# Expert layers of a six-layer network: tokens sorted by expert into 7 blocks of 128, results stored in two transfers

## The reference

```
x = x + 0.5 * ffn(ln(x));  x = x + linear(ln(x));  x = x + 0.5 * ffn(ln(x))
x = x + 0.5 * experts(ln(x));  x = x + attn(ln(x));  x = x + 0.5 * experts(ln(x))
```

```
probs = softmax(q k^T * 8**-0.5)                  # 16 heads, 256 x 256 per sequence
x = layer_norm(src + (probs v) @ Wo + bo)
expert_idx = floor(x @ router_w + router_b) mod 4
for e in range(4):
    y = relu(x @ W1[e] + b1[e]) @ W2[e] + b2[e]
    ff_out += where(expert_idx == e, y, 0)
return layer_norm(x + ff_out)
```

## Time and profile before

| | |
|---|---|
| runs | 1931.28, 1931.81, 1939.92 us |
| profiled execution, its time | 1933.48 us |
| its span | 1931.3 us |
| TensorE matmul busy | 1437.2 us (74%), 10336 matmuls |
| TensorE weight load busy | 860.4 us (45%), beside the matmuls |
| VectorE busy | 1356.9 us (70%) |
| ScalarE busy | 724.2 us (37%) |
| GpSimd busy | 615.0 us (32%) |
| mean granted clock of TensorE | 0.864 |
| DMA | 62.16 MB |

### The profile page before, as it was taken

One profiled execution on the slowest core, in us unless ns is written; L12 is line 12 of the kernel. 1 busy time (PEld: TensorE's weight loads), 2 busy tenths in 40 slices (PEclk: granted clock), 3 DMA queues, 4 the chain that ended last, 5 costly groups with the idle time before them and its releaser, 6 DMA issues.

```text
span 1931.3 us, 30180 instructions
## 1 busy us (share of the span) xinstructions
PE 1437.2 (74%) x10336; PEld 860.4 (45%) x10336; DVE 1356.9 (70%) x3522; ACT 724.2 (37%) x1329; POOL 615.0 (32%) x464
## 2 busy tenths in 40 slices
PE   3667667656643557988899996665467889989997
PEld 3334334333431223555555664444123455555665
DVE  6699999999873646766776456884665567767554
ACT  1233323333110234555555531222043455555642
POOL 3245445545552201222121123664121122321211
PEclk9887888788755578999999997787576999999999
DMA  4000000000002212211120000001221102210000
GB/s 143 0 1 1 1 0 0 1 0 1 1 2 66 74 61 68 68 51 51 35 68 3 1 1 1 1 0 39 85 75 51 58 28 68 67 52 18 24 12 11
DMA packets 73541, 62.16 MB, mean 32 GB/s; under 512 B 4920, under 2 KB 66488, under 8 KB 73272
## 3 DMA queue, kind: packets, MB, share of 16 engines
q1 hardware_dynamic: 73408, 60.48, 10.0%
HBM read 32.61 MB, written 27.79 MB: 31 GB/s over the span
## 4 chain that ended last, share of the span: by engine, by line
PE 51%; DVE 27%; issue 12%; POOL 4%; DMA 2%; SPq 2%; ACT 1%; DVEq 1%; POOLq 0%; ACTq 0%
PE bank L1073 12%; PE bank L1065 11%; PE bank L1087 7%; DVE DD L1349 6%; PE bank L1103 4%; DVE NM L1578 4%; PE bank L1116 3%; PE bank L955 2%; PE bank L1125 2%; DVE A L1360 2%; PE bank L1136 1%; DVE YB L1491 1%; PE bank L1131 1%; PE bank L1199 1%; POOL rs L582 1%
## 5 line engine op out<-in xcount | busy, mean ns | idle before, releaser
L1578 DVE TENSOR_REDUCE NM<-bank 128x2 f32<-128x512 f32 x512 | 342.5, 685 | 270.2 <-PE bank L1116 269.3
L836 ACT ACTIVATE PBS<-bank 128x512 f32<-128x512 f32 x512 | 289.4, 597 | 393.1 <-PE bank L1103 392.9
L1073 PEld LDWEIGHTS bank<-W,HB 128*128 128x128 f32 x2048 | 264.1, 191 | 157.2 <-issue 135.6
L582 POOL TENSOR_TENSOR rs<-ve,half 128x4 f32<-128x4 f32 x88 | 90.2, 1025 | 707.4 <-DVE ve L1518 587.8
L1073 PE MATMUL bank<-W,HB 128*128 128x128 f32 x2048 | 272.4, 276 | 24.6 <-DVE YB L1491 24.6
L1065 PE MATMUL bank<-XT,W 128*128 128x512 f32 x512 | 284.8, 638 | 1.1 <-ACT HB L808 1.1
L1349 DVE TENSOR_TENSOR_SCAN DD<-bank,I 128x512 f32<-128x512 f32 x192 | 227.1, 1209 | 11.6 <-PE bank L943 9.2
L808 ACT ACTIVATE HB<-bank,W 128x512 f32<-128x512 f32 x256 | 176.5, 690 | 129.3 <-PE bank L1065 128.3
L943 PE MATMUL bank<-STK,SEL 128*128 128x256 bf16 (+1 forms) x512 | 87.5, 281 | 132.3 <-DVE DD L1349 130.7
L1116 PE MATMUL bank<-KS,QS 48*128 48x256 bf16 x1024 | 113.0, 303 | 79.9 <-DVE NM L1578 51.9
L616 POOL TENSOR_TENSOR A<-DD,SS 128x512 f32<-128x512 f32 x64 | 98.6, 1541 | 171.3 <-DVE DD L1349 171.2
(11 more groups left out here) (211 smaller groups left out, 2321.0 us busy)
## 6 DMA issues: line engine op xcount, KB each, us to landing
QS<-scr_q SPq DMA_DIRECT2D x64, 192.0 KB
KS<-scr_k SPq DMA_DIRECT2D x64, 192.0 KB
scr_q<-PQ SPq DMA_DIRECT2D x32, 192.0 KB, 2.2
scr_k<-PQ SPq DMA_DIRECT2D x32, 192.0 KB, 2.2
scr_q<-PQ SPq DMA_DIRECT2D x32, 128.0 KB, 2.1
scr_k<-PQ SPq DMA_DIRECT2D x32, 128.0 KB, 2.1
X<-in_x SPq DMA_DIRECT2D x8, 256.0 KB, 6.6
W<-in_w SPq DMA_DIRECT2D x8, 256.0 KB, 8.3
```

The costliest lines, as they stand in the source:

```text
L582: pool.tensor_tensor(rs_[:, :], ve_[:, :], half[:, 0:ve_.shape[1]], ALU.pow).then_inc(rstd_sem, 1)
L836: act.activation(PB[i % PB_SLOTS][:, :, :], bank[1 + i % 2][:, :].rearrange("p (k t) -> p k t", k=2), ACT.Exp).then_inc(A.e, 1)
L1073: last = pe.matmul(bank[7][:, k * P:(k + 1) * P], HB[e % 2][:, q, k * P:(k + 1) * P], W2[:, e, q, :], start=(q == 0), stop=(q == CH - 1))
L1578: dve.tensor_reduce(NM[:, 2 * b + qt, h:h + 3:2], bank[3 + i % 2][:, :].rearrange("p (u t) -> p u t", u=2), AX_X, ALU.max, negate=True).th ...
```

## The change

The experts no longer work on all 512 tokens with each expert. The tokens of a group are sorted by expert into 7 blocks of 128 tokens. Blocks 0 to 3 belong to the four experts and use the weights that stand in SBUF (resident blocks). An expert with more than 128 tokens fills further blocks, of which there are three (overflow blocks); (512 - 4) // 128 = 3 is the largest number that can be needed. What weights an overflow block needs is known only at run time, so they are fetched.

- At the start SyncE packs the weights and biases of each expert into a table in HBM, `scr_w`: for each expert 128 rows of 1156 numbers.
- VectorE's `choose` takes the place of `masks`, in slot 26 and not 27, behind the new `take(., 0)`. It ends with one comparison that gives `hot`, one column for each expert. TensorE's `count_ranks` in slot 29 (five small products with a triangle and with ones) counts the rank of each token in its expert and the tokens of each expert. VectorE's `positions` in slot 31 (14 small operations) works out the row of each token (POS) and the rows of the three overflow blocks' weights (WIX).
- In the next step Pool scatters the four tiles of XS into `scr_x` by POS (four indirect transfers), SyncE loads it back sorted as XD, TensorE transposes its seven blocks in slot 15, and ScalarE copies them to XT. Pool also gathers the overflow blocks' weights from `scr_w` into WK (three indirect transfers).
- In the odd slots from 17 on TensorE makes `up` of a block (four products of 128 columns) and `down` of the block before (four accumulating ones); ScalarE makes the Relu of a block in four operations. `take(., 0)` in slot 26 adds the biases of the resident blocks, `take(., 1)` in slot 1 of the following step those of the overflow blocks. SyncE stores the results of the two parts to `scr_y` by separate transfers: the one of the resident blocks behind slot 26's take, that of the overflow blocks behind slot 1's.
- Pool gathers the results back in token order into YG (four indirect transfers), and VectorE adds them to XS in slot 10 of the step with `fin`.
- The loop over the full steps is written out. Twenty-two constants and a running sum of the identity are set by VectorE when the engines' program comes to the first expert layer's setup, which stands between the linear-attention layer and the second feed-forward layer. The buffers KQV of the attention lie over WK, some semaphores of the feed-forward layer and the attention are shared, and one lead of the attention moves from slot 26 to 28.

The diff, cut to its core:

```diff
-UNITS = [None] * SLOTS_H
-for _e in range(EXPERTS):
-    for _k in range(CH):
-        for _kind, _slot in (("W1", 8 * _e + 2 * _k - 2), ("W2", 8 * _e + 2 * _k + 7)):
-            UNITS[_slot % SLOTS_H] = (3 + _slot // SLOTS_H, _kind, _e, _k)
...
+OVER = (N - EXPERTS) // P
+BLOCKS = EXPERTS + OVER
...
+def first_slot(b):
+    return 17 + 2 * b
...
+            for e in range(EXPERTS):
...
+                sp.dma_start(scr_w[r, 0:W2_AT], W1[:, e, :]).then_inc(E.packed, 16)
+                sp.dma_start(scr_w[r, W2_AT:B1_AT],
+                             W2[:, e, :, :].rearrange("p k c -> p (k c)")).then_inc(E.packed, 16)
...
+                    if fin:
+                        sp.wait_ge(E.yused, 2 * (c - 3))
+                        sp.dma_start(scr_y[EXPERTS * P:, :].rearrange("(b p) c -> p b c", p=P),
+                                     YB[:, EXPERTS:, :]).then_inc(E.ystored, 16)
...
+                    if exp:
+                        sp.wait_ge(E.scattered, 64 * (c - 2))
...
+                        sp.dma_start(XD[:, :, :], scr_x.rearrange("(b p) c -> p b c", p=P)).then_inc(E.sorted, 16)
...
+                    if exp:
+                        sp.wait_ge(E.yused, 2 * (c - 2) - 1)
...
+                        sp.dma_start(scr_y[0:EXPERTS * P, :].rearrange("(b p) c -> p b c", p=P),
+                                     YB[:, 0:EXPERTS, :]).then_inc(E.ystored, 16)
...
+                    if exp:
+                        pool.wait_ge(E.pos, c - 2)
...
+                        for t in range(TP):
+                            pool.indirect_dma_start(
+                                out=scr_x, out_offset=bass.IndirectOffsetOnAxis(ap=POS[other][:, t:t + 1], axis=0),
+                                in_=XS[other][:, t, :], in_offset=None).then_inc(E.scattered, 16)
+                    if fin:
...
+                        for t in range(TP):
+                            pool.indirect_dma_start(
+                                out=YG[:, t, :], out_offset=None, in_=scr_y,
+                                in_offset=bass.IndirectOffsetOnAxis(ap=POS[par][:, t:t + 1], axis=0)
...
+                    if exp:
...
+                        for k in range(OVER):
+                            pool.indirect_dma_start(
+                                out=WD[:, k, :], out_offset=None, in_=scr_w,
+                                in_offset=bass.IndirectOffsetOnAxis(ap=WIX[other][:, k:k + 1], axis=0)
+                                ).then_inc(E.weights, 16)
...
+                        if exp and i in (15, 16):
...
+                            act.activation(XT[:, at:to], bank[6 + u][:, 0:to - at], ACT.Copy).then_inc(E.xt, 1)
+                        if exp and i in range(first_slot(0), first_slot(BLOCKS), 2):
+                            relu(n - 3, (i - first_slot(0)) // 2)
...
-                def unit(p, kind, e, k):
...
-                    if kind == "W1":
...
-                        pe.matmul(bank[6][:, :], W1[:, e, k * P:(k + 1) * P], XT[:, :], start=True,
-                                  stop=True).then_inc(E.h, 1)
-                        return
...
+                def up(p, b):
...
+                    if b == EXPERTS:
+                        pe.wait_ge(E.weights, 16 * OVER * (c + 1))
+                    for k in range(CH):
+                        w = W1[:, b, k * P:(k + 1) * P] if b < EXPERTS else WD[:, b - EXPERTS, k * P:(k + 1) * P]
+                        last = pe.matmul(bank[6][:, k * P:(k + 1) * P], w, XT[:, b * P:(b + 1) * P], start=True, stop=True)
...
+                def down(p, b):
...
+                    pe.wait_ge(E.relu, c * BLOCKS + b + 1)
+                    if b == 0:
+                        pe.wait_ge(E.xt, 2 * c + 2)
+                    if b == EXPERTS:
+                        pe.wait_ge(E.yused, 2 * c + 1)
+                    for k in range(CH):
+                        at = W2_AT + k * P
+                        w = W2[:, b, k, :] if b < EXPERTS else WD[:, b - EXPERTS, at:at + P]
+                        last = pe.matmul(bank[7][:, (b % EXPERTS) * P:(b % EXPERTS + 1) * P], HB[b % 2][:, k, :], w,
+                                         start=(k == 0), stop=(k == CH - 1))
+                    last.then_inc(E.y, 1)
...
+                def count_ranks():
...
+                    pe.matmul(bank[0][:, 0:n], below[:, :], h, start=True, stop=False)
+                    for t in range(1, TP + 1):
+                        last = pe.matmul(bank[0][:, t * EXPERTS:n], allone[:, :], h[:, 0:n - t * EXPERTS],
+                                         start=False, stop=(t == TP))
...
+                            b2 = (i - first_slot(0)) // 2
+                            if exp and 0 <= b2 < BLOCKS:
+                                up(n - 3, b2)
+                            if exp and 0 < b2 <= BLOCKS:
+                                down(n - 3, b2 - 1)
+                            if exp and i == 15:
...
+                                        last = pe.transpose(bank[6 + u][:, k * P:(k + 1) * P], XD[:, at + k, :], ident)
+                                    last.then_inc(E.turned, 1)
...
+                        if post and i == 29:
...
-                            pe.wait_ge(A.x1, c - 1)
-                            turn(XS[par], E.turned)
+                            pe.wait_ge(E.hot, c - 1)
...
+                            count_ranks()
...
+                def take(p, u):
...
+                        dve.tensor_tensor(YB[:, 0:EXPERTS, :], tiles(7), R[:, k:k + EXPERTS, :],
...
+                        dve.wait_ge(E.y, c * BLOCKS + BLOCKS)
+                        dve.wait_ge(E.weights, 16 * OVER * (c + 1))
+                        dve.tensor_tensor(YB[:, EXPERTS:BLOCKS, :], tiles(7)[:, 0:OVER, :], WD[:, :, B2_AT:WROW],
+                                          ALU.add).then_inc(E.yused, 1)
...
+                def choose(p, par):
...
-                    for e in range(EXPERTS):
-                        last = dve.tensor_scalar(MK[par][:, e, :], key[2][:, :], float(e), None, ALU.is_equal)
-                    last.then_inc(E.mask, 1)
+                    dve.tensor_tensor(hot[:, 0:TP, :], over(key[2][:, :].unsqueeze(2), [P, TP, EXPERTS]),
+                                      expert_no[:, :, :], ALU.is_equal).then_inc(E.hot, 1)
+                    link.close()
...
+                def positions(p, par):
...
+                    dve.wait_ge(E.rank, c + 1)
+                    ranks = bank[0][:, 0:TP * EXPERTS].rearrange("p (t e) -> p t e", e=EXPERTS)
+                    counts = bank[0][:, TP * EXPERTS:(TP + 1) * EXPERTS]
+                    link(dve.tensor_tensor(full[:, :, :], over(counts.unsqueeze(2), [P, EXPERTS, OVER]),
+                                           filled[:, :, :], ALU.is_gt))
+                    link(dve.tensor_reduce(extra[:, :], full[:, :, :], AX_X, ALU.add))
...
+                    dve.tensor_scalar(WIX[par][:, :], owner[:, :], part_no[:, 0:1], None, ALU.add)
...
+                    dve.tensor_copy(POS[par][:, :], spot[:, :]).then_inc(E.pos, 1)
...
-                        if fin and i == 6:
-                            take(n - 4, 3)
-                        if fin and i == 7:
-                            gather(n - 4, par, 3)
+                        if fin and i == 1:
+                            take(n - 4, 1)
+                        if fin and i == 10:
+                            dve.wait_ge(E.back, 64 * (c - 3))
+                            if later(c - 4):
+                                dve.wait_ge(E.norm, c - 4)
+                            dve.tensor_tensor(AC[:, :, :], XS[par][:, :, :], YG[:, :, :], ALU.add).then_inc(E.acc, 1)
...
-                        if exp and i == 14:
-                            take(n - 3, 0)
...
-                        if exp and i == 17:
-                            gather(n - 3, other, 0)
-                        if exp and i == 22:
-                            take(n - 3, 1)
-                        if exp and i == 23:
-                            gather(n - 3, other, 1)
...
-                        if post and i == 27:
-                            masks(n - 2, par, (c - 2) * 4 - 2)
-                        if exp and i == 30:
-                            take(n - 3, 2)
-                        if exp and i == 31:
-                            gather(n - 3, other, 2)
+                        if exp and i == 26:
+                            take(n - 3, 0)
+                        if post and i == 26:
+                            choose(n - 2, par)
+                        if post and i == 31:
+                            positions(n - 2, par)
```

279 lines of the change are left out of this document (176 added, 103 removed).

## The result

The changed kernel takes 2003.97 us, the median of four runs (2003.24 to 2005.84). Its time over that of the kernel before is 1.0362, with a 95% interval of 1.0335 to 1.0389: slower by 71 us, in the direction forecast, at nearly twice the size (+37). It lies inside the range given (1885 to 2040) and outside the narrower one that the forecast gave for itself (1945 to 1995). The profiled execution has a span of 2001.5 us against 1931.3, and a mean clock of 0.768 against 0.864. TensorE's matmuls are busy for 1323.9 us, 113 less than before.

What follows compares the result with a forecast made beforehand. TensorE bounds full steps now; without expert work, a chain through one PSUM bank would pace the first half. First layer +14.9, second +19.9, constants +2.5 made +37: 1969 us, range 1885 to 2040 (forecast's own 1945 to 1995).

Steps and rivals of the forecast that it cites:

- What bounds, first half: Slots 0 to 15 of a full step: without expert work, a chain through one PSUM bank paces it; 37.2 us.
- less 1.3: First half of a full step: 1.3 us taken off because the step is entered at the full clock.
- Second half: Slots 16 to 31 of a full step: 27.8 us with VectorE's stalls, plus 2.4 for lost clock, giving 30.2.
- the stall in slot 28: Maxima of slot 28 wait for both reduces, take and choose: 3.3 us exposed on TensorE.
- Full steps together: Each full step goes from 61.5 to 67.4 us, +5.9, four times in each layer: +23.6 per layer.
- Tails: Ends of layers: -4.7 us for the sorted-load step; then 0 in the first layer, +5 in the second.
- The step behind the last maxima: First step after the last maxima, paced by exponentials and one block per pair: 39.3 us, -7.
- The constants: 22 memsets and a few small VectorE operations between the linear layer and second ffn: +2.5 us.
- The steps that only choose: Steps that only choose: +2 us, from positions and choose ahead of the reduce, less one W1 unit.
- Pool late: Rival, chance 0.14: at 2.3 us per transfer, qkr and all behind it come 6 us late; 2035 us.
- TensorE's bound: Rival, chance 0.03: TensorE stays the bound, so 16.7 us go from each of 16 passes; 1665 us.
- The clock holds: Rival, chance 0.22: halves at their floors, 29.8 and 27.8, make a full step 57.6 us; total 1883 us.

Runs made afterwards that it cites:

- the first experiment: Changed kernel plus one unread 512-column TensorE product in each odd slot 1 to 13 of steps 2 to 7: 1892.37 us, ratio 0.9789 to the kernel before.

## Why the prediction was right, and where it was too low

**What bounds, first half.** Right, and its cause is shown: the half went to 39.2 us at a clock of 0.61 where 37.2 at 0.6 to 0.75 was forecast, and giving TensorE work took it to 30.0 with all waits in place. What was mis-sized is the base. Of the two measured stretches without expert work I took the shorter, 37.7 at 0.68; with the other, 39.5 at 0.59, the same sum gives 39.0. That they differ at all is the clock, as the 32.0 at 0.93 shows, and the changed kernel's clock of 0.61 is that of the longer one. The step was entered at the full clock, as the term "less 1.3" has it; whether that gave anything no run separates. Neither of the forecast waits ahead of it is by itself what lowered the clock: without the wait for POS in slot 1 the half had 0.58, and without the dip of slot 28 it had 0.61.

**Second half.** 30.2 forecast, 29.4 measured (30.8 in step 6). Its sum of 27.8 at the full clock is what the first experiment shows (27.9). Of the stall in slot 28, put at 3.3, the later `choose` gave 2.1 back at the full clock and 1.6 more in clock; of the 2.7 for `positions`, its removal gave 2.0 there. The 2.4 that I had added for lost clock came as 1.5. The reason that I gave for them, that a stall costs clock, holds only in part: the same wait in slot 28 cost none in the first experiment.

**Full steps together.** +5.9 was forecast eight times, +7.1 to +9.3 came: 16 us of the 33 that were missing. The steps with `exp` but no `fin` (+8.3 and +9.3) have a first half of 40.3 and 41.2 us, and I had given them the value of the others; they are the ones entered at the lower level (0.59 us for the transposes of slot 1, 0.38 in the others). Step 6 (+8.4 twice) has a second half of 30.8, with a longer dip behind slot 28.

**Tails.** Here the step of the sum that failed is the last group. For the second layer behind 1909.6, -4.7 and +5 were put and -2.6 and +11.6 came: 36.2 to 33.6 us (31.5 forecast, whose terms as given add up to 31.2), then 46.7 to 58.3. After, in time order, TensorE and then Pool and VectorE:

```profile
1942.06 1.16 PE L1172 MATMUL bank<-WK,HB 128*128 128x128 f32 x8 [0.23 <-ACT HB L898]
1954.80 1.76 PE L1278 MATMUL bank<-W,XD 128*128 128x128 f32 x7 [11.59 <-DMA XD<-scr_x]
1956.61 2.07 PE L1158 MATMUL bank<-XT,W 128*128 128x128 f32 x8
1960.00 2.05 PE L1158 MATMUL bank<-XT,W 128*128 128x128 f32 x8 [1.32 <-ACT HB L898]
...
1976.10 1.16 PE L1172 MATMUL bank<-WK,HB 128*128 128x128 f32 x8 [0.34 <-ACT HB L898]
```

```profile
1980.62 1.04 POOL L714 DMA_INDIRECT YG<-scr_y,POS  x1 [17.23 <-DMA scr_y<-YB]
```

```profile
1988.27 0.69 DVE L1781 TENSOR_TENSOR AC<-XS,YG 128x512 f32<-128x512 f32 x1 [10.42 <-DMA YG<-scr_y,POS]
```

The way from POS to the sorted load is paid for each group, the last one too; I had counted it once, in the step ahead, and for the last group only store and gathers. From POS (1944.3) to the transposes it is 10.5 us, close to the 4.6 + 2.2 + 3 of the forecast. The seven blocks take from 1956.6 to 1977.3, which is 20.6 and not 16.1: the first three start 3.4, 3.5 and 2.9 us apart, since behind 11.6 idle us the clock is at its lower level, the later ones 2.45. Store and gathers take 11 us from 1977.3 to 1988.3, against 9.3. In the first layer the lead steps of the attention filled part of this, but not all: -7.6 came where -11.7 was put.

**The step behind the last maxima.** -7 forecast, -4.9 measured (46.3 to 41.4).

**Small terms.** The constants, +2.5, cost nothing: all up to the first expert layer took 0.6 us less. The steps that only choose, +2, took +3.7 and +1.1. The second layer's lead steps gave +3.5 that no step of the sum had, and whose cause is not shown.

**Rivals.** Pool late: out, with 7.09 us to spare and six more transfers free. TensorE's bound: out. The clock holds: it did not, but it gives the right price of a full step: with the clock held by hand that is 57.9, and the rival had 57.6. That its total of 1883 stands beside 1892 is luck in part: the products also took 16 us off the two steps that only choose, for which the rival had +4, and the tails came about as much worse than it had them.

**The skill's rules.** The Trainium skill (TensorE: Matmul & The Clock Gate, "Part 1: The HAM clock gate") calls the half rate the default that activity releases; by that rule the half from which TensorE's work was taken could lose the full clock, and the traces agree: 0.61 without, 1.00 with the products that nobody reads. Pool's transfers took 0.93 to 1.09 us each with VectorE busy beside them, and not near the 2.3 us at which I had put them under the shared port. The Trainium skill (SBUF — State Buffer, "Who interferes with whom") says of `tensor_reduce` that on this chip it never contends for that port. I had left that out: beside the eleven transfers of the step shown, reduces are 4.8 of VectorE's 8.4 busy us, so that this case hardly tests the lock.

## What to carry to other kernels

Work that fills an engine's gaps on a chain of hand-overs may be holding its clock up; before it is taken out or pushed together, look for a stretch of the same kernel that lacks it and read its time and its clock there. Then price what is left at both levels: here the sum of 29.8 was the answer with the clock (30.0), and the two stretches of 37.7 and 39.5 held the one without it (39.2) between them. An idle stretch of the other engine is not room for new work if what ends it is a link of the chain, and a transfer that is hidden in the steady state is paid in full for the last group.

## What the runs showed of the hardware

- One unread product of 1.02 to 1.13 us in each of seven gaps took the clock of the half from 0.61 to 1.00 and a step from 68.6 to 57.9 us. With 8 columns in place of 512 it left the clock of step 2 at 0.59, against 0.94 and 0.95.
- A W2 unit of 8 columns took 1.04 us at the full clock, one of 128 columns 1.05, eight matmuls each: fewer columns made it no shorter.
- In a full step an indirect transfer of 128 rows occupied Pool for 0.93 to 1.09 us and 0.30 more to the next, whether its rows had 512 bytes or 4.6 KB.
- In three kernels with indirect transfers on the second chip ScalarE and VectorE waited up to 10.6 and 11.8 us at a time, mostly in slot 6, for an unseen releaser. Open.
